# A macaron of two attentions and four feed-forward layers: the order of TensorE's work within one attention step

## What is computed

```python
attn = jnp.einsum('bhqd,bhkd->bhqk', q, k) * scale
attn = jax.nn.softmax(attn, axis=-1)
out = jnp.einsum('bhqk,bhkd->bhqd', attn, v)
out = out.transpose(0, 2, 1, 3).reshape(B, S, INNER)
return out @ Wo + bo
```

## Time and profile before

| what | value |
| --- | --- |
| executions, us | 2328.54, 2326.64, 2328.67 |
| the profiled execution, us | 2328.73 |
| its span from first to last instruction, us | 2326.9 |
| granted TensorE clock, mean over the span | 0.987 |
| TensorE busy, us | 2259.0 (97%) |
| DVE busy, us | 1612.8 (69%) |
| ACT busy, us | 1136.9 (49%) |
| POOL busy, us | 830.5 (36%) |
| first and last transpose of the attention, us | 650.2 and 1740.4 |

### The profile page before, as it was taken

The page is one execution under the profiler, slowest core; times in us unless marked ns, Lnnn a source line. Parts: engine busy times, 40 slices in busy tenths (PEclk is TensorE's granted clock), DMA queues, the critical chain, the costliest instruction groups (busy, mean ns, idle before and its releaser), DMA issues. The chain is left out here.

```text
span 2326.9 us, 34378 instructions
## 1 busy us (share of the span) xinstructions
PE 2259.0 (97%) x11044; PEld 1876.6 (81%) x11044; DVE 1612.8 (69%) x2655; ACT 1136.9 (49%) x1846; POOL 830.5 (36%) x736
## 2 busy tenths in 40 slices
PE   7899999999989999999999999999999999899998
PEld 5688888888768888888888888888886788687886
DVE  5644444444378888888888888888885666784765
ACT  3233323332266666666666666666663344352442
POOL 4543332233222222212212222222214466672565
PEclk9999999999999999999999999999999999898999
DMA  3255555455332211211221221221201111040210
GB/s 95 74 177 195 189 174 185 166 187 185 132 102 75 81 54 68 81 64 58 81 72 50 81 72 50 81 81 46 76 24 41 50 68 44 33 130 36 73 59 37
DMA packets 106326, 210.99 MB, mean 91 GB/s; under 512 B 9744, under 2 KB 42512, under 8 KB 102928
## 3 DMA queue, kind: packets, MB, share of 16 engines
q1 hardware_dynamic: 106256, 210.10, 26.8%
HBM read 140.86 MB, written 69.21 MB: 90 GB/s over the span
## 5 line engine op out<-in xcount | busy, mean ns | idle before, releaser
L1069 ACT ACTIVATE at_pT_hi<-ps 128x512 fp32r<-128x512 f32 x512 | 278.4, 596 | 351.9 <-PE ps L1173 351.8
L1111 DVE TENSOR_REDUCE at_small<-ps 128x1 f32<-128x1024 f32 x256 | 312.7, 1221 | 88.6 <-PE ps L360 87.8
L1121 DVE TENSOR_TENSOR at_pT_lo<-ps,at_pT_hi 128x512 fp32r<-128x512 f32 x512 | 327.3, 681 | 2.2 <-ACT at_pT_hi L1069 2.2
L1076 ACT ACTIVATE at_probs<-ps,at_small,cols 128x1024 f32<-128x1024 f32 x256 | 309.3, 1208 | 28.9 <-DVE at_small L1113 23.0
L826 POOL TENSOR_TENSOR qkv_acc<-qkv_acc,qkv_sq 128x512 f32<-128x512 f32 x128 | 166.4, 1300 | 322.3 <-ACT qkv_sq L715 318.9
L1173 PEld LDWEIGHTS ps<-ident,at_probs 128*128 128x128 f32 x2048 | 238.4, 140 | 37.9 <-issue 4.2
L1173 PE MATMUL ps<-ident,at_probs 128*128 128x128 f32 x2048 | 265.7, 272 | 2.6 <-DVE at_pT_lo L1121 2.6
L360 PE MATMUL ps<-ln_xT_hi,qkv_w_hi 128*128 128x512 f32 x496 | 194.2, 391 | 9.1 <-DVE qkv_res L787 9.1
L1006 POOL TENSOR_TENSOR at_o_lo<-at_o_raw,at_o_hi 128x512 fp32r<-128x512 f32 x32 | 41.3, 1292 | 439.4 <-ACT at_o_hi L1090 439.4
L1135 DVE SCALAR_TENSOR_TENSOR x<-ps,at_small,x 128x512 f32<-128x512 f32 x256 | 192.1, 751 | 8.0 <-PE ps L360 3.1
L360 PE MATMUL ps<-ln_xT_hi,ln_xT_lo 128*128 128x512 f32 x768 | 196.0, 390 | 0.0
(11 more groups left out here) (263 smaller groups left out, 5267.8 us busy)
## 6 DMA issues: line engine op xcount, KB each, us to landing
scratch_q_hi<-qkv_q_hi SPq DMA_DIRECT2D x64, 256.0 KB, 2.0
scratch_q_lo<-qkv_q_lo SPq DMA_DIRECT2D x64, 256.0 KB, 2.3
scratch_k<-qkv_res SPq DMA_DIRECT2D x64, 256.0 KB, 2.6
scratch_v<-qkv_res SPq DMA_DIRECT2D x64, 256.0 KB, 2.3
k_raw<-scratch_k SPq DMA_DIRECT2D x32, 512.0 KB, 3.5
at_v_raw<-scratch_v SPq DMA_DIRECT2D x32, 512.0 KB, 3.3
qkv_w<-in_Wq SPq DMA_DIRECT2D x8, 1024.0 KB, 6.3
qkv_w<-in_Wk SPq DMA_DIRECT2D x8, 1024.0 KB, 5.0
```

The costliest lines, as they stand in the source:

```text
L1069: nc.scalar.activation(pT2[jp][0][:, 4 * b:4 * b + 4, w * P:(w + 1) * P], T_BANKS[:, b * HALF:(b + 1) * HALF].rearrange("p (k n) -> p k n" ...
L1076: nc.scalar.activation(probs[l % 4][:], scores(l)[:], ACT.Exp, bias=nbias[:, l % 4:l % 4 + 1], scale=rq[:, l % NT:l % NT + 1], accum_out=s ...
L1111: nc.vector.reduce_max(maxes[:, l % 4:l % 4 + 1], scores(l)[:], AX.X).then_inc(s_max, 1)
L1121: nc.vector.tensor_tensor(pT2[jp][1][out], T_BANKS[:, b * HALF:(b + 1) * HALF].rearrange("p (k n) -> p k n", k=4), pT2[jp][0][out], ALU.su ...
```

## The change

The six score matmuls of a step are cut into two threes, and the eight transposes into two fours. The order becomes: scores of keys 0 to 511, transposes of the first four blocks of tile p - 2, scores of keys 512 to 1023 with the signal `s_scores`, the other four transposes, and then the output product and the second product as before. The helper `turn` issues four transposes with their wait for `s_pT_lo` and their signal `s_T`. The waits keep their values; the programs of the other engines are untouched.

```diff
--- before.py
+++ after.py
@@ -1146,6 +1146,13 @@
 
         @block.tensor
         def _(pe):
+            def turn(l, q, b):
+                wait(pe, s_pT_lo, 2 * (q - 1) + b + 1)
+                for k in range(4 * b, 4 * b + 4):
+                    last = nc.tensor.transpose(T_BANKS[:, k * P:(k + 1) * P],
+                                               probs[(l - T_LAG) % 4][:, k * P:(k + 1) * P], core.ident[:])
+                last.then_inc(s_T, 1)
+
             def step(i, l):
                 p = BODY * i + l
                 if exists(i, l):
@@ -1160,19 +1167,15 @@
                         wait(pe, q_in[hp], 32 * (i + hp))
                     wait(pe, s_exp, p - 1)
                     s = slice(qt * P, (qt + 1) * P)
-                    for n in range(NH):
-                        m = slice(n * HALF, (n + 1) * HALF)
-                        last = product(nc, scores(l)[:, m], [((qh[:, s], ql[:, s]), (kh[:, m], kl[:, m]))])
-                    last.then_inc(s_scores, 1)
+                    product(nc, scores(l)[:, 0:HALF], [((qh[:, s], ql[:, s]), (kh[:, 0:HALF], kl[:, 0:HALF]))])
                 if exists(i, l, T_LAG):
-                    q = p - T_LAG
-                    pe.wait_ge(s_exp, q + 1)
-                    for b in range(2):
-                        wait(pe, s_pT_lo, 2 * (q - 1) + b + 1)
-                        for k in range(4 * b, 4 * b + 4):
-                            last = nc.tensor.transpose(T_BANKS[:, k * P:(k + 1) * P],
-                                                       probs[(l - T_LAG) % 4][:, k * P:(k + 1) * P], core.ident[:])
-                        last.then_inc(s_T, 1)
+                    pe.wait_ge(s_exp, p - T_LAG + 1)
+                    turn(l, p - T_LAG, 0)
+                if exists(i, l):
+                    product(nc, scores(l)[:, HALF:TOK], [((qh[:, s], ql[:, s]), (kh[:, HALF:TOK], kl[:, HALF:TOK]))])\
+                        .then_inc(s_scores, 1)
+                if exists(i, l, T_LAG):
+                    turn(l, p - T_LAG, 1)
                 if exists(i, l, WO_LAG):
                     J, jp, hp, w = lagging(i, l, WO_LAG)
                     if w == 0:
```

## The result

The changed kernel takes 2334.67 us (median of 7 runs), the kernel before 2328.67 us in the 7 runs beside it: 1.0031 of it, with a 95% interval of 1.0019 to 1.0043, that is 4 to 10 us more. The forecast was 2334.3, slower.

The account below looks back on a forecast made before the run. TensorE's own instruction stream was taken as the bound, 4.306 us a step. Terms 2.5 + 0.3 + 2.2 + 0.4 + 0.4 = +5.8 took 2328.73 us to 2334.5, median 2334.3; range 2330.0 to 2341.5.

Parts of the forecast that it names:

- the likeliest case: Whole kernel: the terms sum to +5.8 us, giving a median of 2334.3 us; chance 0.45.
- (a): Each step: first four transposes come 0.68 us earlier, the scores' signal and the maximum behind it 0.44 us later.
- (b): Steady part, TensorE itself: one more entry and exit of a transpose run, 0.010 us for 249 steps, +2.5 us.
- (c): Steady part, waits: transposes free; output product behind the next head's K split short by 0.01 us, 31 heads, +0.3 us.
- (d): Start, steps 3 to 6: a new loop makes the cycle between maxima 3.52 us instead of 2.90, +2.2 us.
- (e): Step 10: the second product's wait for `y_lo` grows, +0.4 us.
- (f): End, step 256: the output product waits for the addition, which hangs on the last exponential, +0.4 us.
- a free steady part: Rival: steady part costs nothing, only start, step 10 and end are paid, +3.0 us, 2331.5 us; chance 0.31.
- the wait of the output product behind the K split: Rival: chain 0.2 us later than read, a new wait in 31 heads, 6.2 us more, 2340.5 us; chance 0.08.
- a doubled aftermath: Rival, steady part: each transpose run costs its aftermath again, +11 us in place of 2.5, 2342.8 us; chance 0.07.
- The fall of the clock: Rival, start: TensorE's clock falls to 1.2 GHz, slowing score matmuls in four cycles, +2.4 us, 2336.7 us; chance 0.05.

Follow-up runs that it names:

- stalled variant: All eight transposes put ahead of all six score matmuls, old order in steps 0 to 7, against the kernel before: 2455.49 us, ratio 1.0547.
- one-signal kernel: Changed order with the old start, both transpose signals given by the last transpose: 2333.52 us, ratio 1.0029 to the kernel before.
- the repeat: The changed kernel measured once more, unaltered, beside the kernel before: 2334.47 us against 2325.77, ratio 1.0032.
- the kernel with the late second run: Second four transposes moved behind the output product, old order in steps 0 to 7, against the kernel before: 2346.01 us, ratio 1.0077.

## Why the prediction was right, step by step

The direction and the likeliest case came out, and the size: 2334.67 measured, 2334.3 forecast. That the two lie within 0.4 us is in part luck, as the terms show:

- **(a)** held: the maximum moved with the end of the scores by four transposes.
- **(b)** had part of the mechanism and half the size. I took 0.010 us for a second run from its entry and its exit; the step grew by 0.020 (1052.16 - 1047.32 = 4.84 over 243 steps), in the changed kernel and in both kernels that have its steady order. The entry and the exit are there and cost a little more than the 4 and 5 ns that I read: averaged over the steps of the trace before, 0.233 us where 0.226 is due and 0.342 where 0.335 is. What I missed is that behind a run the next few 512-column matmuls are slow too, 0.23 or more in place of 0.226. The starts of a step of the slower kind in the trace before show it, 0.23, 0.23 and 0.24 apart (0.229, 0.233 and 0.236 in the mean of such steps):

```profile
1208.88 0.39 PE L360 MATMUL ps<-at_o_lo,at_y_hi 128*128 128x512 f32 x1
1209.11 0.40 PE L360 MATMUL ps<-at_o_hi,at_y_lo 128*128 128x512 f32 x1
1209.34 0.40 PE L1198 MATMUL ps<-at_pT_hi,at_v_hi 128*128 128x512 f32 x1
1209.58 0.39 PE L1198 MATMUL ps<-at_pT_lo,at_v_hi 128*128 128x512 f32 x1
```

I had argued them away with the two kinds of step, 4.29 and 4.33, which have one run each. Averaged over the trace they are 4.297 and 4.323, so they differ by 0.025 and not by 0.04. After the change that alternation is gone, and the steps take 4.327 except behind the split of K. Why they alternate before, and why that ends, no run shows. The term was +2.5 and measured +5.0 for 249 steps, with what (c) has in it. (Only from step 12 on does a step have the output product, so there are 244 with all parts and not 249; that makes 0.1 us.) The upper bound, the whole 0.044 doubled, was too much.
- **(c)** named the right place, the step behind the split of K, and the wrong wait. The output product doesn't wait there. In the timeline of the changed kernel:

```profile
1131.02 0.69 DVE L1107 TENSOR_TENSOR at_y_lo<-ps,at_y_hi 128x512 fp32r<-128x512 f32 x1 [0.49 <-ACT at_y_hi L1061]
...
1131.14 0.48 PE L360 MATMUL ps<-at_o_hi,at_y_hi 128*128 128x512 f32 x1
...
1131.83 0.19 PEld L1201 LDWEIGHTS ps<-at_pT_hi,at_v_hi 128*128 128x128 f32 x1 [0.18 <-issue]
1131.92 0.41 PE L1201 MATMUL ps<-at_pT_hi,at_v_hi 128*128 128x512 f32 x1
...
1134.65 0.75 DVE L1135 SCALAR_TENSOR_TENSOR x<-ps,at_small,x 128x512 f32<-128x512 f32 x1
...
1135.50 0.48 PE L360 MATMUL ps<-at_o_hi,at_y_hi 128*128 128x512 f32 x1
```

The addition is over at 1135.40 and the output product starts at 1135.50: 0.10 us, where 0.12 was forecast. It starts as soon as the transposes ahead of it let it. What does wait is the first weight load of the second product, for which I had said that `y_lo` has room. `y_lo` is over at 1131.71, 0.21 before the matmul at 1131.92; but a weight load runs some 0.23 ahead of its matmul, and this one stands 0.18 us and starts 0.12 behind `y_lo`. The view names no releaser for it; that it is `y_lo` follows from the program's wait and from this distance, which is the same in every head. It is the row of 14 waits shown at the top, one in every second head, in all profiles with the new steady order and in none with the old one. The step there takes 4.36 us (1131.14 to 1135.50) for 4.33: some 0.01 of that is the late matmul, the rest slower matmuls behind it, whose cause stays open. Over the attention the steps behind the split of K cost 0.5 to 0.7 us by the four profiles of the new steady order, where this term had +0.3.
- **(d)** had the mechanism and the cycle: 3.52 forecast, 3.57 measured, and the stalled variant above shows the same loop in the steady part. The size was a little low. With 24.93 and 24.94 us (the first of them with a fall of the clock in it) against 21.6 to 22.5 in the six kernels with the old start (21.62, 22.48, 21.64, 22.04, 21.78 and that of the one-signal kernel, 22.04; mean 21.93) the maximum of step 7 comes 3.0 us later, of which 0.44 are the shift of the scores itself: 2.6 on the path, for 2.2. The old starts alone differ by 0.9 us, so the 2.6 is known to some 0.4 either way; most of their difference lies between the maxima of steps 2 and 3 (3.85 to 4.42 us).
- **(e)** +0.45 for +0.4; the waits in the start, 5.1 and 1.1 us (4.3 and 1.1 in the repeat), are the "some 5" and "near 1.0" that were named. **(f)** +0.45 for +0.4: in step 256 the output product starts 1.53 us behind the first transpose (1743.67 to 1745.20), where it started 1.08 behind it (1736.55 to 1737.63).

The sum by what the runs showed is 5.0 + 2.6 + 0.45 + 0.45 = 8.5, against 4 to 10 by the interval. The forecast of 5.8 was short by 2.7, most of it in (b) and (c), and came close because the medians of the first comparison are only 6.0 us apart; in the repeat they are 8.7 apart, as the sum has it. The parts add up in the ratios as well: 0.21% for the steady part with step 10 and the end, 0.14% for the start, 0.35% together, against 0.31% and 0.32%.

The rivals: a free steady part is out (4.33 with the old start); the wait of the output product behind the K split didn't arise, though it is real, as the kernel with the late second run shows; a doubled aftermath is too large. The fall of the clock did occur in the profiled start, at some 1.8 us for the 2.4 of that rival, but it is not bound to the order: between 650 and 658 us two of the three profiles with the new start have one and one of the seven with the old. Whether the new start makes it more likely isn't shown by so few. The rule of the Trainium skill, "TensorE: Matmul & The Clock Gate", Part 4, by which transposes don't count as activity, isn't needed for it: the start with the new order and its longer waits ran at 1.00 from 650 us on in the kernel that had it alone, and in the steady part, with 0.87 us of transposes in each 4.31, the granted clock is 1.00 as well.

## What to carry to other kernels

Where an engine is busy throughout, moving its instructions gains nothing in the steady part, and what decides is the loops that the new order closes: follow each signal that moved back to its waiter and compare the loop with the step, in the start and the end of the pipeline too, where the step is short. Here the same loop of maximum, low part, transposes and scores was harmless at 3.57 us in a step of 4.33, bound the start, and made every step 4.8 us when all the transposes were put into it. Read the room of a wait against the weight load, which runs ahead of its matmul, and not against the matmul alone. Keep small matmuls in one run: each further run had its price of 10 to 20 ns a step, and over hundreds of steps that was about half of the loss.

## What the runs showed of the hardware

- The price of a second run of transposes doesn't depend on what stands behind it (scores or output product, 4.33 us both ways) nor on when ACT reads the transposed half. Why the few matmuls behind a run take 4 to 9 ns more, and why the step behind the K split has more of them, stays open; no run here separates it from the reads of the other engines in that stretch.
- A weight load that waits shows in the rows of PEld and may not show in those of PE: behind the K split it stood 0.18 us, and its matmul started 0.24 us behind the one ahead, for 0.23.
- In all ten profiles the granted clock is below 1.00 from 642 to 646 us (0.50 to 0.87), about the first maximum. In three it falls again between 650 and 658 us, in either order of the start. In the first profile of the changed kernel this alone was some 26.78 - 24.94 = 1.8 us, a third of the change, in a stretch that a comparison of the two traces would have put down to it entirely.
